# A recurrent stage of 128 steps written out without loops, with root, gate scaling and softmax made for two quads at once

## The chip, the cores and the metric

One core of one Trainium2 chip runs the whole program. The metric is device time in microseconds (us), from launch to the last result, as the median of several executions; lower is better. The profile covers one execution: its span runs from the first to the last instruction and is a little shorter than the device time of the same execution.

## The reference

The input x is 128 batches x 128 tokens x 128 channels, in float32, and adj a 128x128 weight matrix for each batch. Two blocks follow one another:

```python
def step(h, x):
    h = jnp.tanh(x @ Wx + h @ Wh + b)
...
x = x + gnn(layernorm(x), adj)      # gnn: agg = (beta / rowsum(adj)) x adj, then the scan of step over the 128 tokens
x = x + ffn(layernorm(x), ...)
# ffn: gate_logits = x @ gate_w + gate_b; top 2 of 16 experts, softmax over the two;
#      relu(x @ w1[e] + b1[e]) @ w2[e] + b2[e], weighted, added to x, layernorm, gamma, beta
```

The scan is a chain of 128 steps, and each step handles all 128 batches at once (the state h is a 128x128 tile).

## The kernel before, in words

The program has four stages one after the other in time: (1) statistics, scaling and aggregation with adj, by batches, up to about 78 us; (2) the recurrent stage, 78 to about 288 us, which this case is about; (3) a pass of the experts over the rows sorted by first choice; (4) a pass over the rows sorted by second choice.

**The recurrent stage** runs on all five engines, and four tokens make a *quad*, so there are 32 quads (`NQ`). Per quad:

- TensorE (`steps` L449 in the block that begins at L383). Step k of quad q waits for the tanh before it (`s_th`) and multiplies by Wh into a PSUM bank (L455). Behind the four steps other work is put in: behind step 0 the input part of the next quad (`fresh`, L446); behind step 1 `turn_h` of quad q-1, four transposes of h (L408); behind step 2 `count` of quad q-3 (five small matmuls on the one-hots, L437 to L440, which wait for `s_hot`) and then `logits` of quad q-2 (L425); behind step 3 `turn_x` of quad q-1, four transposes (L416, they wait for `s_x1`).
- ScalarE (`steps` L549): the tanh (L554), and behind step 0 the copy of the transposed x (`x1T_out` L529) and `tokens` (L546); behind step 1 `exps` and `sums` of quad q-3 (L535, L539, for the softmax; they wait for `s_dd`); behind steps 2 and 3 a part of the centring of w2.
- VectorE (`turn` L801): everything else of a quad, in 23 parts that are spread over three turns by a table of (part, lag). Turn q takes `tile_a` (L624: h transposed plus the residual x, waits for `s_ht`, for the load of x and for the slot's old scatters), `tile_b`, `tile_b2` (statistics of four tokens, L631, L638), `tile_b3`, `root_0` and eight small parts (one over the root of the variance, L645 to L680) of quad q-1; `gate_1` to `gate_5` (scaled logits, bias, largest values, their indices, one-hots; L693 to L730) of quad q-2; the softmax weights (L738, L742) and `place_1` to `place_3` (the row that each token goes to; L750 to L766) of quad q-3.
- GpSimd (`send` L328, scatter L222): four indirect DMAs a quad write the quad's rows to `rows_by_first` in DRAM. `send` waits for `tokens`, for the weights (`s_w1`) and for the places (`s_d`).
- SP loads the residual x of a quad (L256), four quads ahead: the load of quad q+4 is issued when `tile_a` of quad q is done. Between the loads of quads 4 to 7 and that of quad 8 it issues the filling of `rows_by_second`, w1, b1, gamma and beta.

The tile `st` has eight slots of a quad each: `tile_a` and `tokens` of quad q wait until the scatters of quad q-8 have landed. When the last places are known, VectorE works out tables for the expert passes (L820 to L856); when all engines are done with the stage's block, stage 3 starts.

The loops are these. `quads` (L233) writes the first 8 quads out and runs the other 24 as a hardware loop of 3 rounds with 8 quads each; VectorE, ScalarE and GpSimd use it, TensorE's own loop has 2 rounds between two written-out pieces. In the loop a wait against a number that depends on the round needs a register operation ahead of it, and `hold` puts one more wait on a constant in front.

```python
order = ((tile_a, 1), (soft_2, 3), (tile_b, 1), (soft_3, 3), (place_1, 3), (tile_b2, 1), (place_2, 3),
         (tile_b3, 1), (gate_1, 2), (root_0, 1), (place_3, 3), (sq_0, 1), (gate_2, 2),
         (ag_0, 1), (gate_3, 2), (in_0, 1), (gate_4, 2), (ou_0, 1), (sq_1, 1), (gate_5, 2), (ag_1, 1),
         (in_1, 1), (ou_1, 1))
```

In the profile L233 is the loop, and L222 the scatter of all stages.

Of the kernel before, what the change touches and what calls it, by code (L numbers as in the profile page):

```python
# [13 lines left out]
P = 128  # L14
# [3 lines left out]
UN = 4  # L18
GNN_EPS = 1e-7
# [15 lines left out]
def build(nc, x, adj, eW, Wx, Wh, b, gate_w, gate_b, w1, b1, w2, b2, gamma, beta, out):  # L35
# [11 lines left out]
    with ExitStack() as ctx:  # L47
# [73 lines left out]
        dd = fsb("dd", [P, 2, QUAD])  # L121
        ex = fsb("ex", [P, 2, QUAD])
        den = fsb("den", [P, 2, QUAD])
# [10 lines left out]
        ve2 = fsb("ve2", [P, 2, QUAD])  # L134
        root_y = fsb("root_y", [P, 2, QUAD])
        root_a = fsb("root_a", [P, 2, QUAD])
        root_b = fsb("root_b", [P, 2, QUAD])
        lgs = fsb("lgs", [P, 2, QUAD, NE])
        mx8 = fsb("mx8", [P, 2, QUAD, 8])
        ix8 = fsb("ix8", [P, 2, QUAD, 8], U32)  # L140
# [149 lines left out]
        def _(pool):  # L290
# [93 lines left out]
        def _(pe):  # L384
# [35 lines left out]
            def logits(q, u):  # L420
                pe.wait_ge(s_xe, q + 1)
                if beyond(q, 1):
                    pe.wait_ge(s_l1, q)
                for j in range(QUAD):
                    i = mm(ps_lg[:, j * NE:(j + 1) * NE], x1T[:, u % 2, j * P:(j + 1) * P], gwc[:, :],  # L425
# [23 lines left out]
            def steps(q, u):  # L449

                for k in range(QUAD):
# [29 lines left out]
            count(NQ - 3, UN - 3)  # L481
            logits(NQ - 2, UN - 2)
            turn_x(NQ - 1, SLOTS - 1)
            logits(NQ - 1, UN - 1)
            count(NQ - 2, UN - 2)
            count(NQ - 1, UN - 1)
# [9 lines left out]
        def _(act):  # L496
# [34 lines left out]
            def exps(q, u):  # L531
                act.wait_ge(s_dd, q + 1)
                if beyond(q, 2):
                    act.wait_ge(s_w1, q - 1)
                a(ex[:, u % 2, :], dd[:, u % 2, :], ACT.Exp).then_inc(s_ex, 1)  # L535

            def sums(q, u):
                act.wait_ge(s_ex, q + 1)
                a(den[:, u % 2, :], ex[:, u % 2, :], ACT.Identity, bias=unit[:, :]).then_inc(s_den, 1)  # L539
# [9 lines left out]
            def steps(q, u):  # L549
                for k in range(QUAD):  # L550
# [34 lines left out]
            quads(act, steps, SLOTS)  # L585
            exps(NQ - 3, UN - 3)
            sums(NQ - 3, UN - 3)
            x1T_out(NQ - 2, UN - 2)
            x1T_out(NQ - 1, UN - 1)
            exps(NQ - 2, UN - 2)  # L590
            sums(NQ - 2, UN - 2)
            exps(NQ - 1, UN - 1)
            sums(NQ - 1, UN - 1)
# [5 lines left out]
        def _(dve):  # L599
# [41 lines left out]
            def tile_b3(q, u):  # L641
                dve.wait_ge(s_pr, q + 1)
                if beyond(q, 2):
                    dve.wait_ge(s_r2, q - 1)
# [569 lines left out]
```

## Time and profile before

| | us |
|---|---|
| device time, median of 3 runs | 710.54 (709.33 to 710.82) |
| device time of the profiled execution | 710.99 |
| its span | 709.0 |
| recurrent stage: first tanh to last tanh | 77.89 to 260.84 |
| first and last scatter to `rows_by_first` begin | 97.29 and 283.59 |
| first instruction of stage 3 | 288.10 |

Busy shares of the whole span: TensorE matmuls 77%, weight loads 69%, VectorE 76%, ScalarE 58%, GpSimd 66%. The mean granted clock of TensorE is 0.888 of full speed. Shares over the whole span mix four stages with different limits, so for this change only views cut to the stage say something: who waits for whom, busy time by window, and instructions in order of time. In such a timeline the distance between the starts of two neighbours on one engine is what the first of them costs that engine, and it can be smaller than its duration, since neighbours overlap.

### The profile page before, as it was taken

The numbers are of one execution on the slowest core, as the hardware profiler recorded it, in microseconds if no ns is written. First come the engines' busy times: TensorE is split into PE (matmuls) and PEld (weight loads), VectorE is DVE, ScalarE is ACT, GpSimd is POOL, SyncE is SP. The second block draws the span as 40 slices with busy tenths as digits, with TensorE's granted clock in tenths as the row PEclk, the third lists the DMA queues.
The fourth block names the chain that finished last, engine by engine and source line by source line (L and its number), as shares of the span: only waits on it lengthen the run. The fifth ranks groups of instructions, "written<-read, shape, count | busy, mean of one in ns | idle before, by whom it ended". The sixth has DMA issues, their size and how long they took to land.

```text
span 709.0 us, 18043 instructions
## 1 busy us (share of the span) xinstructions
PE 544.5 (77%) x4140; PEld 486.8 (69%) x4140; DVE 539.0 (76%) x2791; ACT 407.8 (58%) x1345; POOL 466.6 (66%) x526
## 2 busy tenths in 40 slices
PE   1766789887888873399999999800799999999920
PEld 1655566665666652399999999800789999999920
DVE  5988599897997997288888888700299999999950
ACT  2889655454554540266666666500588888888810
POOL 3666647675765767067777777776067777777774
PEclk9989999897987985599999999955799999999975
DMA  8999649432332313379885665430997676664110
GB/s 216 282 281 282 158 147 278 143 104 75 96 94 84 97 49 114 80 210 334 258 251 192 202 190 185 150 149 28 294 328 231 191 215 202 208 203 142 49 49 7
DMA packets 115098, 121.40 MB, mean 171 GB/s; under 512 B 19017, under 2 KB 99613, under 8 KB 115008
## 3 DMA queue, kind: packets, MB, share of 16 engines
q1 hardware_dynamic: 95936, 76.79, 38.7%
q0 software_dynamic: 17920, 43.03, 16.7%
q8 instruction: 34, 0.56, 0.4%
q10 hardware_dynamic: 1152, 0.56, 0.3%
q14 instruction: 56, 0.46, 0.2%
HBM read 68.67 MB, written 55.90 MB: 176 GB/s over the span
## 4 chain that ended last, share of the span: by engine, by line
PE 38%; POOL 7%; ACT 7%; issue 4%; DMA 1%; DVE 1%; SPq 1%; POOLq 0%; ACTq 0%; DVEq 0%
PE bank L987 19%; PE bank L1003 15%; ACT hs L1055 4%; POOL rows_by_second L222 4%; POOL out_dram L222 3%; PE bank L976 3%; ACT xT L1036 2%; PE bank L1000 2%; DMA R<-rows_by_second 0%; DMA rows_by_second<-R 0%; DMA R<-rows_by_first 0%; ACT wr L1044 0%; SPq L912 0%; ACT L1064 0%; SPq L914 0%
## 5 line engine op out<-in xcount | busy, mean ns | idle before, releaser
L222 POOL DMA_INDIRECT rows_by_second<-R x144 | 146.2, 1015 | 62.2 <-issue 36.6
L222 POOL DMA_INDIRECT out_dram<-R x144 | 143.2, 994 | 66.7 <-issue 38.7
L1055 ACT ACTIVATE hs<-bank,wr 128x128 f32<-128x128 f32 x432 | 127.5, 368 | 86.7 <-PE bank L987 82.7
L1003 PE MATMUL bank<-W,hs 128*128 x1152 | 176.1, 289 | 0.0
L222 POOL DMA_INDIRECT rows_by_first<-st x128 | 125.3, 979 | 76.6 <-ACT st L546 40.2
L987 PE MATMUL bank<-xT,wr 128*128 128x128 f32 x1152 | 159.1, 282 | 7.2 <-ACT xT L1036 6.7
L1003 PEld LDWEIGHTS bank<-W,hs 128*128 128x128 f32 x1152 | 151.7, 192 | 3.5
L987 PEld LDWEIGHTS bank<-xT,wr 128*128 128x128 f32 x1152 | 143.1, 196 | 14.6 <-ACT xT L1036 13.4
L1124 DVE SCALAR_TENSOR_TENSOR R<-bank,R 128x128 f32<-128x128 f32 x288 | 87.6, 346 | 66.6 <-PE bank L1003 63.2
L1044 ACT COPY wr<-W1b 128x258 f32 x288 | 105.0, 427 | 14.7 <-PEq L858 14.7
L554 ACT ACTIVATE HT<-bank,bcol 128x128 f32<-128x128 f32 x128 | 46.7, 365 | 69.6 <-PE bank L455 65.7
L976 PE MATMUL bank<-ident,R 128*128 128x128 f32 x288 | 45.0, 281 | 54.0 <-DMA R<-rows_by_second 40.9
L976 PEld LDWEIGHTS bank<-ident,R 128*128 128x128 f32 x288 | 35.1, 146 | 54.7 <-DMA R<-rows_by_second 41.1
L1036 ACT COPY xT<-bank 128x512 f32<-128x512 f32 x72 | 42.9, 595 | 47.7 <-PE bank L976 47.7
L455 PEld LDWEIGHTS bank<-HT,Wh_sb 128*128 128x128 f32 x254 | 45.8, 212 | 35.0 <-ACT HT L554 29.7
L455 PE MATMUL bank<-HT,Wh_sb 128*128 128x128 f32 x254 | 62.3, 331 | 3.3 <-ACT HT L554 2.3
L1000 PE MATMUL bank<-b2s,sel 128*128 128x128 bf16 x288 | 63.2, 219 | 0.4 <-ACT hs L1055 0.3
L400 PE MATMUL bank<-aq,xs 128*128 128x128 f32 x256 | 42.2, 319 | 24.9 <-ACT xs L511 24.8
L400 PEld LDWEIGHTS bank<-aq,xs 128*128 128x128 f32 x256 | 36.4, 221 | 30.7 <-ACT xs L511 19.2
L1113 DVE TENSOR_SCALAR hs<-bank,wr 128x128 f32<-128x128 f32 x144 | 43.8, 346 | 10.3 <-PE bank L987 10.3
L1102 DVE TENSOR_SCALAR R<-R 128x128 f32<-128x128 f32 x144 | 42.2, 366 | 11.7 <-DMA R<-rows_by_first 11.7
L511 ACT ACTIVATE xs<-xq,scq 128x128 f32<-128x128 f32 x128 | 40.8, 391 | 10.0 <-POOL scq L325 9.1
(137 smaller groups left out, 875.4 us busy)
## 6 DMA issues: line engine op xcount, KB each, us to landing
R<-rows_by_second SPq DMA_DIRECT2D x144, 196.0 KB
R<-rows_by_first SPq DMA_DIRECT2D x144, 68.0 KB
xq<-in_x_dram SPq DMA_DIRECT2D x32, 256.0 KB, 4.0
aq<-in_adj_dram SPq DMA_DIRECT2D x32, 256.0 KB, 5.0
x2r<-in_x_dram SPq DMA_DIRECT2D x32, 256.0 KB, 2.9
rows_by_second<-filler SPq DMA_DIRECT2D x1, 3136.0 KB, 13.7
rows_by_second<-filler SPq DMA_DIRECT2D x16, 196.0 KB
rows_by_second<-R POOLq DMA_INDIRECT x144
```

The lines of the kernel that those rows point to most:

```text
L222: return nc.gpsimd.indirect_dma_start(dst, bass.IndirectOffsetOnAxis(ap=idx, axis=0), src, None, bounds_check=limit[n], oob_is_err=False)
L400: i = mm(ps_agg[u % 2][:, j * P:(j + 1) * P], xs[:, u % 2, j * P:(j + 1) * P], aq[:, u, j * P:(j + 1) * P], start=True, stop=True)
L455: mm(ps_rnn[u % 2][:, k * P:(k + 1) * P], Wh_sb[:, :], HT[:, h, ((k - 1) % QUAD) * P:((k - 1) % QUAD + 1) * P], start=False, stop=True, sk ...
L554: a(HT[:, u % 2, k * P:(k + 1) * P], ps_rnn[u % 2][:, k * P:(k + 1) * P], ACT.Tanh, bias=bcol[:, :]).then_inc(s_th, 1)
L976: i = nc.tensor.transpose(ps_z[:, j * P:(j + 1) * P], R[:, u, j, C_Z:C_Y], ident[:, :])
L987: i = mm(ps_h[c][h][:, (j % 2) * P:(j % 2 + 1) * P], wr[:, u % 2, j, c * P:(c + 1) * P], xT[:, u % 2, j * P:(j + 1) * P], start=True, stop ...
L1000: mm(o, sel[:, bass.ds(e[k], 1), :].rearrange("p o m -> p (o m)"), b2s[:, :], start=True, stop=False, skip_group_check=True)
L1003: i = mm(o, hs[:, h, c, k * P:(k + 1) * P], W2[:, bass.ds(e[k], 1), c, :].rearrange("p o f -> p (o f)"), start=False, stop=c == 1, skip_gr ...
L1036: nc.scalar.copy(xT[:, u % 2, :], ps_z[:, :]).then_inc(e_xe, 1)
L1044: i = nc.scalar.copy(wr[:, u % 2, j, :], W1b[:, bass.ds(e, 1), :].rearrange("p o f -> p (o f)"))
L1055: i = a(hs[:, h, c, k * P:(k + 1) * P], ps_h[c][h][:, k * P:(k + 1) * P], ACT.Relu, bias=wr[:, u % 2, 2 * h + k, F + c:F + c + 1])
L1124: i = v.scalar_tensor_tensor(out=y, in0=ps_o[h][:, k * P:(k + 1) * P], scalar=R[:, u, j, w:w + 1], in1=y if r else R[:, u, j, C_Z:C_Y], op ...
```

## The change

TensorE, ScalarE, VectorE and GpSimd write out all 32 quads of the stage, with no loop. `tile_b3`, the root, `gate_1` to `gate_3`, the difference for the softmax (now `apart`) and the softmax weights are made once for a pair of quads, with tiles twice as wide. VectorE's table of parts is replaced by two kinds of turn, `even` and `odd`: the root of a pair is made in the even turn t = 2p+2, the gate of the pair in the odd turn 2p+3, the indices and one-hots of quad q in turn q+3 (before: q+2), the places of quad q in turn q+4 (before: q+3). TensorE takes the logits behind step 1 instead of step 2, and the counts of quad q-4 instead of q-3. ScalarE's exp and sum are made once a pair, in even quads. Cut to its core:

```diff
@@ pool
-                pool.wait_ge(s_w1, q + 1)
+                pool.wait_ge(s_w1, q // 2 + 1)
...
-            def turn(q, u):
-                if beyond(q, 3):
-                    send(q - 3, (u - 3) % SLOTS)
-            quads(pool, turn, SLOTS)
-            for k in range(3):
-                send(NQ - 3 + k, SLOTS - 3 + k)
+            for q in range(NQ):
+                send(q, q % SLOTS)
@@ pe
-                if beyond(q, 1):
-                    pe.wait_ge(s_l1, q)
+                if beyond(q, 2):
+                    pe.wait_ge(s_l1, q // 2)
...
-                    if k == 2 and beyond(q, 3):
-                        count(q - 3, u - 3)
-                    if k == 2 and beyond(q, 2):
+                    if k == 1 and beyond(q, 2):
                         logits(q - 2, u - 2)
+                    if k == 2 and beyond(q, 4):
+                        count(q - 4, u - 4)
...
-            for u in range(SLOTS):
-                steps(u, u)
-            with pe.Fori(1, NQ // SLOTS - 1) as J:
-                for u in range(SLOTS):
-                    steps(SLOTS * J + u, u)
-            for u in range(SLOTS):
-                steps(NQ - SLOTS + u, u)
+            for q in range(NQ):
+                steps(q, q % SLOTS)
@@ act
-                    if k == 1 and beyond(q, 3):
-                        exps(q - 3, u - 3)
-                        sums(q - 3, u - 3)
+                    if k == 1 and q % 2 == 0 and q > 3:
+                        exps(q // 2 - 2)
+                        sums(q // 2 - 2)
...
-            quads(act, steps, SLOTS)
+            for q in range(NQ):
+                steps(q, q % SLOTS)
@@ dve (root, gate_1 to gate_3, apart, soft_2, soft_3: one call a pair, 8 columns for 4)
-                v.tensor_scalar(ve2[:, u % 2, :], st[:, u, :, C_RSTD], LN_EPS, None, ALU.add).then_inc(s_v2, 1)
+                v.tensor_scalar(ve2[:, p % 2, :], two(p, C_RSTD), LN_EPS, None, ALU.add).then_inc(s_v2, 1)
...
-                v.tensor_tensor(lgs[:, h, :, :], ps_lg[:, 0:QUAD * NE].rearrange("p (i e) -> p i e", i=QUAD),
+                v.tensor_tensor(lgs[:, p % 2, :, :], ps_lg[:, 0:PAIR * NE].rearrange("p (i e) -> p i e", i=PAIR),
...
-            quads(dve, turn, SLOTS)
-            for q in range(NQ, NQ + 3):
-                turn(q, q % SLOTS)
+            def odd(t):
+                p = (t - 3) // 2
+                one(tile_a, t - 1)
+                one(tile_b, t - 1)
+                pair(gate_1, p)
+                one(tile_b2, t - 1)
+                pair(gate_2, p)
+                one(place_1, t - 4)
+                pair(gate_3, p)
+                one(place_2, t - 4)
+                pair(apart, p)
+                one(gate_4, t - 3)
+                one(place_3, t - 4)
+                one(gate_5, t - 3)
+
+            def even(t):
+                p = (t - 2) // 2
+                one(tile_a, t - 1)
+                one(tile_b, t - 1)
+                one(gate_4, t - 3)
+                one(tile_b2, t - 1)
+                one(gate_5, t - 3)
+                pair(tile_b3, p)
+                one(place_1, t - 4)
+                pair(root_0, p)
+                pair(soft_2, p - 1)
+                pair(sq_0, p)
+                one(place_2, t - 4)
+                pair(ag_0, p)
+                pair(soft_3, p - 1)
+                pair(in_0, p)
+                one(place_3, t - 4)
+                pair(ou_0, p)
+                pair(sq_1, p)
+                pair(ag_1, p)
+                pair(in_1, p)
+                pair(ou_1, p)
+
+            for t in range(0, NQ + 4, 2):
+                even(t)
+                odd(t + 1)
```

How this moves instructions, at three places. TensorE, one quad of the stage before, from the transposes of h behind step 1 to the input part of the next quad (L455 is a step, L437 to L440 the count, L425 the logits, L416 the transposes of x):

```order
L408 MATMUL bank<-ident,HT 128x128 [waits s_x1]
L408 MATMUL bank<-ident,HT 128x128 x3
L455 MATMUL bank<-HT,Wh_sb 128x128 [waits s_th]
L437 MATMUL bank<-hot,ones 128x160 [waits s_hot]
L438 MATMUL bank<-hot,tri 128x128
L440 MATMUL bank<-hot,ones 128x96
L440 MATMUL bank<-hot,ones 128x64
L440 MATMUL bank<-hot,ones 128x32
L425 MATMUL bank<-gwc,x1T 128x16 [waits s_l1,s_xe]
L425 MATMUL bank<-gwc,x1T 128x16 x3
L455 MATMUL bank<-HT,Wh_sb 128x128 [waits s_th]
L416 MATMUL bank<-ident,st 128x128 [waits s_xe,s_x1]
```

The same piece of a quad in the change (L454 is a step, L424 the logits, L436 to L439 the count, L414 the transposes of x):

```order
L406 MATMUL bank<-ident,HT 128x128 [waits s_x1]
L406 MATMUL bank<-ident,HT 128x128 x3
L424 MATMUL bank<-gwc,x1T 128x16 [waits s_l1,s_xe]
L424 MATMUL bank<-gwc,x1T 128x16 x3
L454 MATMUL bank<-HT,Wh_sb 128x128 [waits s_th]
L436 MATMUL bank<-hot,ones 128x160 [waits s_hot]
L437 MATMUL bank<-hot,tri 128x128
L439 MATMUL bank<-hot,ones 128x96
L439 MATMUL bank<-hot,ones 128x64
L439 MATMUL bank<-hot,ones 128x32
L454 MATMUL bank<-HT,Wh_sb 128x128 [waits s_th]
L414 MATMUL bank<-ident,st 128x128 [waits s_xe,s_x1]
```

The logits now stand ahead of step 2 rather than ahead of step 3, and the count stands alone behind step 2. VectorE, the gate inside a turn of the loop before (L710 finds the largest values, L718 their indices, L722 is the difference; root parts between them):

```order
L663 REGISTER_ALU
L664 TENSOR_TENSOR root_b<-root_a,ve 128x4 [waits s_root]
L710 MAX mx<-lgs 128x8 [waits s_const,s_l2,s_hot]
L710 MAX mx<-lgs 128x8 x3
L670 REGISTER_ALU
L671 SCALAR_TENSOR_TENSOR root_a<-root_b 128x4 [waits s_root]
L718 MAX_INDEX ix<-mx,lgs 128x8 [waits s_mx,s_const]
L718 MAX_INDEX ix<-mx,lgs 128x8 x3
L722 TENSOR_TENSOR dd<-mx 128x4 [waits s_ex]
L678 REGISTER_ALU
L680 SCALAR_TENSOR_TENSOR root_y<-root_a,root_y 128x4 [waits s_root]
```

VectorE in the change, the gate inside an odd turn (L753, L764 and L769 are the places, L708 the largest values, L717 the difference, L724 the indices, L733 the one-hots):

```order
L697 TENSOR_TENSOR lgs<-lgs,gb_bc 128x128 [waits s_l1]
L753 TENSOR_TENSOR posr<-bank,posr 128x160 [waits s_sel,s_cnt]
L708 MAX mx<-lgs 128x8 [waits s_l2,s_hot]
L708 MAX mx<-lgs 128x8 x7
L764 TENSOR_TENSOR picked<-posr,hot 128x128 [waits s_d,s_pos]
L717 TENSOR_TENSOR dd<-mx 128x8 [waits s_ex,s_mx]
L724 MAX_INDEX ix<-mx,lgs 128x8 [waits s_mx]
L724 MAX_INDEX ix<-mx,lgs 128x8 x3
L769 TENSOR_REDUCE st<-picked 128x4x2 [waits s_sel]
L733 TENSOR_TENSOR hot<-ix,iota_e 128x128 [waits s_cnt,s_ix]
```

The register operations are gone, the gate has eight maxima in one go, and no root part stands in the odd turn. All of the root is in the even turn, whose end is (L661 to L677 are the last root parts, L616 is `tile_a` of the next turn):

```order
L745 TENSOR_TENSOR st<-st,ex 128x8 [waits s_red]
L668 SCALAR_TENSOR_TENSOR root_a<-root_b 128x8 [waits s_root]
L769 TENSOR_REDUCE st<-picked 128x4x2 [waits s_sel]
L677 SCALAR_TENSOR_TENSOR root_y<-root_a,root_y 128x8 [waits s_root]
L654 TENSOR_TENSOR root_a<-root_y 128x8 [waits s_root]
L661 TENSOR_TENSOR root_b<-root_a,ve 128x8 [waits s_root]
L668 SCALAR_TENSOR_TENSOR root_a<-root_b 128x8 [waits s_root]
L677 SCALAR_TENSOR_TENSOR st<-root_a,root_y 128x8 [waits s_root]
L616 TENSOR_TENSOR st<-bank,x2r 128x4x128 [waits s_sct2,s_x22,s_ht]
```

The last four root parts follow each other with nothing between them.

## Rows read from the trace of the kernel before

**Rows 1.** Who waited for whom, 78 to 285 us: us in total, times, longest.

```profile
POOL rows_by_first L222 <- ACT st L546: 40.2, 23, 14.6
...
ACT ex L535 <- DVE dd L722: 26.5, 24, 3.1
```

**Rows 2.** Busy by window: PE, PEld, DVE, ACT, POOL, then clock, DMA share, GB/s.

```profile
136.00:159.00 23.00, 18.88 (x127) 14.40 (x127) 21.66 (x167) 12.32 (x46) 16.40 (x17) 0.97 0.33 98
78.00:261.00 183.00, 153.07 (x947) 115.95 (x946) 163.71 (x1192) 93.79 (x343) 113.13 (x114) 0.89 0.39 116
```

**Rows 3.** Timeline of VectorE, one turn: start, duration, line, operation, shapes, [idle before].

```profile
133.90 0.69 DVE L624 TENSOR_TENSOR st<-bank,x2r 128x512 f32<-128x512 f32 x1
...
134.63 0.87 DVE L631 BATCH_NORM_STATS2 bnb<-st 128x6 f32<-128x128 f32 x4
...
135.48 0.32 DVE L750 TENSOR_TENSOR posr<-bank,posr 128x160 f32<-128x160 f32 x1
...
136.00 0.29 DVE L761 TENSOR_TENSOR picked<-posr,hot 128x128 f32<-128x128 f32 x1
136.22 0.16 DVE L645 TENSOR_SCALAR ve<-st 128x4 f32<-128x4 f32 x1
136.29 0.21 DVE L693 TENSOR_TENSOR lgs<-bank,st 128x64 f32<-128x64 f32 x1
136.42 0.15 DVE L650 TENSOR_SCALAR root_y<-ve 128x4 int32<-128x4 int32 x1
...
137.10 0.41 DVE L710 MAX8 mx<-lgs 128x8 f32<-128x16 f32 x4
...
137.61 0.09 DVE L718 MATCH_VALUE_LOAD ix<-mx,lgs 128x8 f32 x1
...
138.21 0.14 DVE L722 TENSOR_TENSOR dd<-mx 128x4 f32<-128x4 f32 x1
...
138.54 0.29 DVE L730 TENSOR_TENSOR hot<-ix,iota_e 128x128 bf16<-128x128 uint32 x1
138.75 0.15 DVE L664 TENSOR_TENSOR root_b<-root_a,ve 128x4 f32<-128x4 f32 x1
138.94 0.16 DVE L671 SCALAR_TENSOR_TENSOR root_a<-root_b 128x4 f32<-128x4 f32 x1
...
139.33 0.69 DVE L624 TENSOR_TENSOR st<-bank,x2r 128x512 f32<-128x512 f32 x1
```

**Rows 4.** Timeline of VectorE: `tile_a` of quads 3, 8 and 15.

```profile
98.70 0.69 DVE L624 TENSOR_TENSOR st<-bank,x2r 128x512 f32<-128x512 f32 x1
...
128.33 0.69 DVE L624 TENSOR_TENSOR st<-bank,x2r 128x512 f32<-128x512 f32 x1 [2.13 <-DMA x2r<-in_x_dram]
...
171.26 0.69 DVE L624 TENSOR_TENSOR st<-bank,x2r 128x512 f32<-128x512 f32 x1 [3.31 <-issue]
```

**Rows 5.** Timeline of GpSimd: the first scatter, the first of quad 6, the last.

```profile
97.29 1.25 POOL L222 DMA_INDIRECT rows_by_first<-st  x1 [14.59 <-ACT st L546]
...
132.14 0.97 POOL L222 DMA_INDIRECT rows_by_first<-st  x1 [2.88 <-ACT st L546]
...
283.59 0.97 POOL L222 DMA_INDIRECT rows_by_first<-st  x1 [0.30 <-issue]
```

**Rows 6.** Timelines of ScalarE and weight loads, quad 8: tanh 0, 1, 3, then the next quad's.

```profile
117.09 0.37 ACT L554 ACTIVATE HT<-bank,bcol 128x128 f32<-128x128 f32 x1 [0.29 <-PE bank L455]
...
118.17 0.37 ACT L554 ACTIVATE HT<-bank,bcol 128x128 f32<-128x128 f32 x1
118.59 0.30 PEld L455 LDWEIGHTS bank<-HT,Wh_sb 128*128 128x128 f32 x2 [0.26 <-ACT HT L554]
...
120.06 0.97 PEld L425 LDWEIGHTS bank<-gwc,x1T 128*128 128x128 f32 x8
...
121.49 0.37 ACT L554 ACTIVATE HT<-bank,bcol 128x128 f32<-128x128 f32 x1 [1.05 <-PE bank L455]
...
122.44 0.37 ACT L554 ACTIVATE HT<-bank,bcol 128x128 f32<-128x128 f32 x1 [0.29 <-PE bank L455]
```

More of the change, by code:

```diff
@@ L18 @@
 UN = 4
+PAIR = 2 * QUAD
+NPAIR = NQ // 2
 GNN_EPS = 1e-7
@@ L584, in _ @@
             agg_out(NQ - 1, UN - 1)
-            quads(act, steps, SLOTS)
-            exps(NQ - 3, UN - 3)
-            sums(NQ - 3, UN - 3)
+            for q in range(NQ):
+                steps(q, q % SLOTS)
             x1T_out(NQ - 2, UN - 2)
             x1T_out(NQ - 1, UN - 1)
[L590 to L593, printed above, removed]
+            for p in range(NPAIR - 2, NPAIR):
+                exps(p)
+                sums(p)
             act.wait_ge(starts, 1)
@@ L639, in tile_b2, with two, tile_b3, root_0 @@
                 i.then_inc(s_pr, 1)
[L641 to L644, printed above, removed]
[L645 to L650 removed]
+            def two(p, c):
+                s = 2 * p % SLOTS
+                return st[:, s:s + 2, :, c].rearrange("p u j -> p (u j)")
+            def tile_b3(p):
+                dve.wait_ge(s_pr, 2 * p + 2)
+                if p > 1:
+                    dve.wait_ge(s_r2, p - 1)
+                v.tensor_scalar(ve2[:, p % 2, :], two(p, C_RSTD), LN_EPS, None, ALU.add).then_inc(s_v2, 1)
+            def root_0(p):
+                dve.wait_ge(s_v2, p + 1)
+                v.tensor_scalar(root_y[:, p % 2, :].bitcast(I32), ve2[:, p % 2, :].bitcast(I32), -0.5, ROOT_BITS,
                                 ALU.mult, ALU.add).then_inc(s_root, 1)
             def square(n):
[L654 to L656 removed]
+                def part(p):
+                    h = p % 2
+                    dve.wait_ge(s_root, 8 * p + 4 * n + 1)
                     v.tensor_tensor(root_a[:, h, :], root_y[:, h, :], root_y[:, h, :], ALU.mult).then_inc(s_root, 1)
@@ L675, in outer, with part @@
             def outer(n, scale):
-                def part(q, u):
-                    h = u % 2
-                    dve.wait_ge(s_root, 8 * q + 4 * n + 4)
+                def part(p):
+                    h = p % 2
+                    dve.wait_ge(s_root, 8 * p + 4 * n + 4)
                     y = root_y[:, h, :]
-                    i = v.scalar_tensor_tensor(out=st[:, u, :, C_RSTD] if n else y, in0=root_a[:, h, :],
+                    i = v.scalar_tensor_tensor(out=two(p, C_RSTD) if n else y, in0=root_a[:, h, :],
                                                scalar=5 * scale ** 4, in1=y, op0=ALU.add, op1=ALU.mult)
@@ L699, in gate_2, with gate_3 @@
+            def gate_2(p):
+                h = p % 2
+                dve.wait_ge(s_l1, p + 1)
                 v.tensor_tensor(lgs[:, h, :, :], lgs[:, h, :, :],
-                                gb_bc[:, :].rearrange("p (o e) -> p o e", o=1).broadcast_to([P, QUAD, NE]),
+                                gb_bc[:, :].rearrange("p (o e) -> p o e", o=1).broadcast_to([P, PAIR, NE]),
                                 ALU.add).then_inc(s_l2, 1)
-            def gate_3(q, u):
-                h = u % 2
-                if beyond(q, 2):
-                    hold(dve, s_hot, q - 1)
-                hold(dve, s_l2, q + 1)
-                for j in range(QUAD):
+            def gate_3(p):
+                h = p % 2
+                if p > 1:
+                    dve.wait_ge(s_hot, 2 * p - 2)
+                dve.wait_ge(s_l2, p + 1)
+                for j in range(PAIR):
@@ L710, in gate_3, with apart @@
                     i = v.max(mx8[:, h, j, :], lgs[:, h, j, :])
                 i.then_inc(s_mx, 1)
+            def apart(p):
+                h = p % 2
+                dve.wait_ge(s_mx, p + 1)
+                if p > 1:
+                    dve.wait_ge(s_ex, p - 1)
+                v.tensor_tensor(dd[:, h, :], mx8[:, h, :, 1], mx8[:, h, :, 0], ALU.subtract).then_inc(s_dd, 1)
             def gate_4(q, u):
-                h = u % 2
-                hold(dve, s_mx, q + 1)
-                for j in range(QUAD):
+                h = q // 2 % 2
+                dve.wait_ge(s_mx, q // 2 + 1)
+                for j in range(q % 2 * QUAD, q % 2 * QUAD + QUAD):
@@ L797, in _, with one, pair @@
             link(v.memset(hot[:, :, 0:2 * NE], 0.0))
-            def turn(q, u):
-                order = ((tile_a, 1), (soft_2, 3), (tile_b, 1), (soft_3, 3), (place_1, 3), (tile_b2, 1), (place_2, 3),
-                         (tile_b3, 1), (gate_1, 2), (root_0, 1), (place_3, 3), (sq_0, 1), (gate_2, 2),
-                         (ag_0, 1), (gate_3, 2), (in_0, 1), (gate_4, 2), (ou_0, 1), (sq_1, 1), (gate_5, 2), (ag_1, 1),
-                         (in_1, 1), (ou_1, 1))
-                for part, lag in order:
-                    if beyond(q, lag) and not (isinstance(q, int) and q - lag >= NQ):
-                        part(q - lag, (u - lag) % SLOTS)
-            quads(dve, turn, SLOTS)
-            for q in range(NQ, NQ + 3):
-                turn(q, q % SLOTS)
+            def one(part, q):
+                if 0 <= q < NQ:
+                    part(q, q % SLOTS)
+            def pair(part, p):
+                if 0 <= p < NPAIR:
+                    part(p)
+            def odd(t):
[37 more added lines that the diff above has]
+                odd(t + 1)
             dve.wait_ge(s_d, NQ)
```

98 lines of the change are left out of this document (44 added, 54 removed).

## The prediction

> **What bounds the kernel now.** I read who waits for whom in the stage first. GpSimd's scatters wait longest for something of their own quad [rows 1], and ScalarE's exp, which stands between two tanh, waits 26.5 us for the difference that VectorE makes. Both point at VectorE. The windows confirm it: in an undisturbed stretch VectorE is busy 21.66 of 23 us (94%), TensorE 18.88, GpSimd 16.40 [rows 2]. The reader is to see that nothing else comes near 94%. The timeline of one turn then gives the period: `tile_a` to `tile_a` is 139.33 - 133.90 = 5.43 us without a gap [rows 3]; over seven turns of the loop it is 171.26 - 128.33 = 42.93, less a gap of 3.31, so 5.66 a turn [rows 4]. That gap has no releaser but "issue" and stands where the loop jumps back; there are two such jumps, since the loop has three rounds. A third gap, 2.13 us, is not the loop's: `tile_a` of quad 8 waits for its load of x [rows 4].
>
> The end of the stage is the last scatter, which begins at 283.59 [rows 5]. A scatter takes 0.97 and the issue behind it 0.30, so 1.27 each and 5.1 a quad. 128 of them need 163 us, but 186.3 lie between the first start and the last [rows 5]; GpSimd is therefore hungry for some 24 us, and that is what this change can win. It is also all that it can win: GpSimd's own work is not touched.
>
> **The new period of VectorE.** I price parts by the distance of starts [rows 3]: `tile_a` until `tile_b` can begin 0.73, `tile_b` with one softmax part 0.85 (0.78 alone), `place_1` with `tile_b2` 0.52, `place_2` 0.20, `tile_b3` 0.07, `gate_1` 0.13, four maxima 0.41, `gate_4` 0.60, one-hots 0.21. `place_3` isn't priced by a row; it is of `place_2`'s kind, 0.20. A small part that needs nothing fresh costs 0.07; one that needs the result of its neighbour costs 0.19 to 0.20 (138.75 to 138.94). Twice the width costs `gate_1` 64 elements more; 512 elements take 0.69 and 64 take 0.21, so 1.07 ns each, and `gate_1` becomes 0.20, `gate_2` 0.21. Eight maxima are 0.70. Eight columns for four in the root cost four elements, nothing that counts.
>
> Even turn: 0.73 + 0.78 + 0.60 + 0.52 + 0.21 + 0.07 = 2.91 up to `root_0`. Then `root_0` to `sq_0` 0.20, `sq_0` 0.07, `place_2` 0.20, `ag_0` to `in_0` 0.20, `in_0` 0.07, `place_3` 0.20: 3.85. Then five root parts with nothing between them, 5 x 0.19 = 0.95: **4.8**. Odd turn: 0.73 + 0.78 + 0.20 + 0.52 + 0.21 + 0.70 + 0.20 + 0.07 + 0.60 + 0.20 + 0.21 = **4.4**. A pair takes 9.2, a turn 4.6. Register operations and the extra constant waits drop out, and the two jumps with them (3.3 each).
>
> **The chain of tanh.** Step 0 to 1 takes 118.17 - 117.09 = 1.08, a step with little behind it 122.44 - 121.49 = 0.95 [rows 6]. The logits move behind step 1: they hold the weight loads for 0.97, of which 0.26 were idle there anyway, so this step takes 0.95 + 0.97 - 0.26 = 1.66. Step 2 keeps the count alone, 0.95, step 3 0.95. Sum 4.64 a quad. exp and sum fit behind tanh 1, once in two quads; the difference they need is made in the odd turn before, over 1 us early. The chain and VectorE now need the same, 4.6 to 4.7 with some friction. Both are below the 5.1 of GpSimd: **GpSimd becomes the bound**, and what is late next is its first scatter and any hole in its supply.
>
> **When the scatters can begin.** Places come a turn later. Quads 0 to 3 of the chain cannot be much faster than before; from 90.5 on they take 4.64, so `tile_a` of quad 3 starts at about 96.6 instead of 98.70 [rows 4]. Turn 4 hands over the places of quad 0 at its 3.9: the first scatter starts at 100.6, 3.3 later than the 97.29 of before [rows 5].
>
> Then comes the load of quad 8. SP issues it behind the filling and w1 to beta, all of it behind `tile_a` of quad 3. From that `tile_a` to the one of quad 8 it is 128.33 - 98.70 = 29.6 [rows 4]. I take this distance as fixed, since SP and the DMA queues set it; it could be shorter at least by the 0.6 to 1 us that is VectorE's, and longer by a few us if scatters and code get in between. VectorE and the chain are there 6 us early and stand still: `tile_a` of quad 8 at 96.6 + 29.6 = 126.2. The same turn hands over the places of quad 5 at its 4.2, so 130.5. GpSimd is through with quad 4 before 127 and stands for some 3.5 us. Before, quad 6 started at 132.14 at this point [rows 5]; now it is quad 5 at 130.5.
>
> From here on a turn (4.7) is shorter than four scatters (5.1), so supply stays ahead. 27 quads are 108 scatters, the last one starts at 130.5 + 107 x 1.277 = 267.1. Two deductions, both allowances: 1.2 us for single slow scatters (the first of the stage took 1.25 instead of 0.97 [rows 5]); and hunger in the first turns after 130.5, while the lead is small, 0.8. The last start is then 269.1 instead of 283.59: **-14.5**. What VectorE does behind the last places (the tables) is hidden behind the last scatters, because those places are ready at 131 + 25 x 4.7 + 4 = 253, 16 us ahead of the last start; without that cover it would lie on the path in full. The way from the last scatter into stage 3, and stages 1, 3 and 4, stay as they are.
>
> **A rule against the change.** An ungrouped turn costs 5.4 [rows 3], more than GpSimd's 5.1, so grouping pays: 25 turns x 0.3 would be lost without it. The Trainium skill (Perfetto Trace Analysis, Optimizing Scalar/DVE Operations) says that grouping helps if the engine is saturated, but where it isn't and only leaves holes in others, "breaking up instructions may allow work to be completed sooner". By the rows VectorE is saturated before the change and isn't after it, so both halves apply: the later places alone cost four scatters, 5.1 us, at the hole at 130.5. By the rule's second half alone the sum would be -19.6, by the rows it is -14.5.
>
> **Rivals.**
> 1. *VectorE or the chain still sets the pace, at 5.1 to 5.7.* For: the mean granted clock of the stage is 0.89, 0.97 in the good window [rows 2], and at half clock the input part and logits grow into the chain; waits now couple two quads. Against: both sums stand 0.5 below. At 5.4 a turn the last places are ready at 131 + 25 x 5.4 + 4.2 = 270, the last scatter starts 3.8 later, -9.6; with 5.7, where only the jumps are won, -2. Time 697 to 709, middle 701. Chance 0.20.
> 2. *The hole at quad 8 is smaller or absent.* If its load comes when VectorE asks for it, GpSimd runs from 100.6 without a hole and the last start is 100.6 + 127 x 1.277 + 2 = 265, or 262.8 with nothing lost: 690 to 692. For: SP's part of the 29.6 isn't shown to be fixed. Against: the wait was a real one before. Chance 0.10.
> 3. *Slower: written-out code does not arrive in time.* A jump cost 3.31 [rows 4]; code that is run once must all be fetched, and if engines stood still for such a gap again and again, the chain would pay each. The result turns to slower when the turns behind quad 8 take over 5.85 on average (131 + 25 x 5.85 + 4.2 + 3.8 = 285), 1.2 more than summed, one gap of 3.3 every third turn. At one every second turn, 6.3 a turn, it is +12, 722. Against: quads 0 to 7, and the first round of the loop, are code that is run for the first time, and up to quad 15 the trace shows only the DMA's gap [rows 4]. Chance 0.04.
>
> **How the numbers follow.** Forecast 0.66, rivals 0.20, 0.10 and 0.04. The profiled execution took 710.99, 0.45 above the median of 710.54; 710.99 - 14.5 = 696.5, against the median 696.0. The forecast's own range comes from the fixed distance (-1 to +3), the hunger (0 to 2) and the friction: 694 to 700. To hold 8 in 10 it reaches down towards rival 2 and up into rival 1: 692.5 to 702.5. A measurement of this kernel tells about 0.2% from no change, 1.4 us. Slower takes rival 3 at 0.04; the same takes the end of rival 1 where next to nothing is won, 0.02; faster 0.94.
>
> **What would show it.** Starts of scatters 1.28 apart from about 130 to the end, with no wait for places or softmax; before 130 one hole of some 3 us. The first scatter near 100.6, `tile_a` of quad 8 near 126 with a DMA as its releaser, the last scatter near 269. VectorE's turns 4.8 and 4.4 where nothing holds them, its busy share well below 94%. Tanh 1 to tanh 2 1.6 to 1.7. No "issue" gap of 3 us. I am wrong if scatters after 131 still wait for places (rival 1), if the hole at quad 8 is missing or twice as long, or if gaps with no releaser recur (rival 3).

## The result and the profile after

| | before | after |
|---|---|---|
| device time, median | 710.48 (709.24 to 710.82, 6 runs) | 693.51 (692.24 to 695.36, 6 runs) |
| ratio to before, 95% interval | 1 | 0.9766 (0.9749 to 0.9783) |
| device time of the profiled execution | 710.99 | 693.63 |
| its span | 709.0 | 691.8 |
| first, last scatter to `rows_by_first` begin | 97.29, 283.59 | 100.89, 266.59 |
| first to last | 186.30 | 165.70 |
| first copy of stage 3 (ScalarE) | 288.67 | 271.67 |

The kernel became 17.0 us faster (median against median), and the last scatter begins 17.0 us earlier. From the first copy of stage 3 to the last instruction both kernels take 420 us (709.0 - 288.67 = 420.3 and 691.8 - 271.67 = 420.1), so the gain lies ahead of stage 3.

Who waits for whom, changed kernel, 78 to 275 us (engine, what it makes and its line, releaser: us in total, times, longest), which answers to [rows 1]:

```profile
ACT HT L548 <- PE bank L454: 53.4, 94, 4.7
...
POOL rows_by_first L224 <- issue: 36.3, 119, 0.3
...
POOL rows_by_first L224 <- ACT st L540: 19.2, 3, 18.6
...
ACT st L540 <- DMA rows_by_first<-st: 10.3, 8, 3.1
...
DVE st L616 <- DMA x2r<-in_x_dram: 4.7, 1, 4.7
...
POOL rows_by_first L224 <- DVE st L769: 3.8, 6, 2.3
```

Of 127 scatters behind the first, 119 now follow the one before them with only the 0.30 of issue (36.3 in 119). The row of 19.2 is nearly all the wait ahead of the first scatter (18.6), and of the 3.8 for places one hole is 2.3. A new row has appeared: ScalarE's `tokens` waits 10.3 us, 8 times, until old scatters have landed. From 182 us on the other engines are so far ahead that the eight slots of `st` are full, and GpSimd holds them back. In the kernel before, GpSimd waited for the others.

The name of the releaser in these rows (`ACT st`, L540 here and L546 in [rows 1]) can't be taken at its word. `send` waits for three semaphores, and `tokens` of the same quad has long run: for quad 0 of the changed kernel at 77.86, for quad 10 of the kernel before at 131.38. What came last is `place_3`. The two engines of the kernel before at quad 10:

```profile
153.31 0.28 DVE L766 TENSOR_REDUCE st<-picked 128x8 int32<-128x128 f32 x1
...
154.40 0.97 POOL L222 DMA_INDIRECT rows_by_first<-st  x1 [0.86 <-ACT st L546]
```

`place_3` ends at 153.59 and the scatter begins 0.81 later. In the kernel before this distance is 0.80 to 1.15 for all quads from 0 to 28, and for nearly all of them GpSimd stands until their places are there. In the changed kernel it is 0.99 at quad 0 and 0.81 at quad 5 (behind the hole), and then it grows: 3.7 at quad 10, 10.2 at quad 20, 17.7 at quad 31. So the places are ready ever earlier than they are needed.

What follows is GpSimd's timeline (start, duration, [idle time before and its releaser]): the first scatter, the hole at quad 5, the last three. They answer to [rows 5].

```profile
100.89 1.25 POOL L224 DMA_INDIRECT rows_by_first<-st  x1 [18.63 <-ACT st L540]
...
125.64 0.97 POOL L224 DMA_INDIRECT rows_by_first<-st  x1 [0.30 <-issue]
128.90 0.97 POOL L224 DMA_INDIRECT rows_by_first<-st  x1 [2.29 <-DVE st L769]
130.17 0.97 POOL L224 DMA_INDIRECT rows_by_first<-st  x1 [0.30 <-issue]
...
264.04 0.97 POOL L224 DMA_INDIRECT rows_by_first<-st  x1 [0.30 <-issue]
265.31 0.97 POOL L224 DMA_INDIRECT rows_by_first<-st  x1 [0.30 <-issue]
266.59 0.97 POOL L224 DMA_INDIRECT rows_by_first<-st  x1 [0.31 <-issue]
```

VectorE's timeline: `tile_a` of quad 3, of quad 8 (with the wait for its load), and the next three, which bound an odd, an even and an odd turn, without their inner parts. They answer to [rows 4] and [rows 3].

```profile
96.01 0.69 DVE L616 TENSOR_TENSOR st<-bank,x2r 128x512 f32<-128x512 f32 x1 [0.40 <-PE bank L406]
...
123.64 0.69 DVE L616 TENSOR_TENSOR st<-bank,x2r 128x512 f32<-128x512 f32 x1 [4.66 <-DMA x2r<-in_x_dram]
...
128.88 0.69 DVE L616 TENSOR_TENSOR st<-bank,x2r 128x512 f32<-128x512 f32 x1 [0.60 <-PE bank L406]
...
133.60 0.69 DVE L616 TENSOR_TENSOR st<-bank,x2r 128x512 f32<-128x512 f32 x1
...
137.94 0.69 DVE L616 TENSOR_TENSOR st<-bank,x2r 128x512 f32<-128x512 f32 x1
```

Even turn 133.60 - 128.88 = 4.72, odd turn 137.94 - 133.60 = 4.34, without a gap of "issue" anywhere.

Four tanh of one quad on ScalarE, and the first of the next (tanh to tanh, as in [rows 6]):

```profile
150.06 0.37 ACT L548 ACTIVATE HT<-bank,bcol 128x128 f32<-128x128 f32 x1 [0.35 <-PE bank L454]
...
151.08 0.37 ACT L548 ACTIVATE HT<-bank,bcol 128x128 f32<-128x128 f32 x1
...
152.63 0.37 ACT L548 ACTIVATE HT<-bank,bcol 128x128 f32<-128x128 f32 x1 [1.19 <-PE bank L454]
...
153.58 0.37 ACT L548 ACTIVATE HT<-bank,bcol 128x128 f32<-128x128 f32 x1 [0.29 <-PE bank L454]
...
154.58 0.37 ACT L548 ACTIVATE HT<-bank,bcol 128x128 f32<-128x128 f32 x1 [0.35 <-PE bank L454]
```

A quad takes 1.02 + 1.55 + 0.95 + 1.00 = 4.52; the 1.55 is the step with the logits behind it.

Busy time by window (length, then busy us of PE, PEld, DVE, ACT, POOL, granted clock, DMA share, GB/s); the first window is the one of [rows 2], the second the hole:

```profile
136.00:159.00 23.00, 21.67 (x158) 17.47 (x159) 22.56 (x173) 14.43 (x52) 17.51 (x19) 1.00 0.40 123
```

```profile
122.00:128.00 6.00, 3.62 (x11) 2.58 (x12) 4.15 (x31) 0.94 (x3) 3.70 (x4) 0.50 0.74 252
159.00:231.00 72.00, 62.95 (x456) 50.28 (x454) 66.45 (x480) 41.21 (x146) 54.93 (x57) 1.00 0.34 101
```

VectorE is busy 98% in the window of [rows 2] and still 92% in the last. So a busy share doesn't tell who bounds here: a VectorE that runs ahead and fills slots is as busy as one that everybody waits for. The waits tell it, and the distance from `place_3` to the scatter.

### The profile page after: what moved, and what is told of

Same layout as the page of the kernel before. It is cut to its first block, busy times and chain, and to the rows that moved or that the text cites. A ratio compares the mean times of both kernels' runs of the same rounds, so it can differ in the third digit from the quotient of the medians.

```text
span 691.8 us, 17131 instructions
## 1 busy us (share of the span) xinstructions
PE 526.6 (76%) x4140; PEld 478.3 (69%) x4140; DVE 511.9 (74%) x2551; ACT 401.5 (58%) x1313; POOL 467.5 (68%) x526
## 4 chain that ended last, share of the span: by engine, by line
PE 38%; ACT 7%; POOL 7%; issue 4%; DVE 2%; DMA 1%; SPq 1%; POOLq 0%; ACTq 0%; DVEq 0%
PE bank L1028 19%; PE bank L1044 15%; POOL rows_by_second L224 5%; ACT hs L1096 5%; PE bank L1017 3%; ACT xT L1077 3%; POOL out_dram L224 2%; PE bank L1041 2%; DMA R<-rows_by_second 1%; DVE R L1197 0%; DVE R L1165 0%; DMA rows_by_second<-R 0%; DMA R<-rows_by_first 0%; DVE R L1189 0%; DVE fst L1175 0%
## 5 line engine op out<-in xcount | busy, mean ns | idle before, releaser
L224 POOL DMA_INDIRECT rows_by_first<-st x128 | 126.0, 984 | 59.3 <-issue 36.3
L454 PE MATMUL bank<-HT,Wh_sb 128*128 128x128 f32 x254 | 58.9, 314 | 15.3 <-ACT HT L548 14.6
L454 PEld LDWEIGHTS bank<-HT,Wh_sb 128*128 128x128 f32 x254 | 41.0, 192 | 42.7 <-ACT HT L548 42.1
```

The costliest lines, as they stand in the source:

```text
L224: return nc.gpsimd.indirect_dma_start(dst, bass.IndirectOffsetOnAxis(ap=idx, axis=0), src, None, bounds_check=limit[n], oob_is_err=False)
L454: mm(ps_rnn[u % 2][:, k * P:(k + 1) * P], Wh_sb[:, :], HT[:, h, ((k - 1) % QUAD) * P:((k - 1) % QUAD + 1) * P], start=False, stop=True, sk ...
```

## The experiments

The expectations speak of four theories. **A**: VectorE set the pace before (turns of 5.4 to 5.7 and the jumps), and after it GpSimd's scatters, 5.1 a quad, once the places are there. **B**: GpSimd bounds both. **C**: VectorE, or the chain of tanh, bounds both. **D**: the pairing is what pays, not the loops.

The experiments ran on four chips. Two of them ran every kernel much slower (the kernel before 904 us instead of 710); what they gave stands apart below. Times elsewhere are from chips where the kernel before takes 709.7 to 710.5.

### More work for GpSimd

A memset of 128 x 392 numbers ahead of the four scatters of each quad, in the kernel before (`before_pool_more`) and in the changed one (`after_pool_more`). In both it waits, with `hold`, for the memset of the quad before.

```diff
+                g.memset(spare[:, :], 0.0).then_inc(s_spare, 1)
                 for j in range(QUAD):
                     scatter(dram_a.ap()
```

> The kernel before with one more GpSimd instruction a quad (a memset of 128x392, 0.42 us where the trace has one) ahead of each quad's scatters. Theory A (before: VectorE's 5.66 us a turn bounds, GpSimd's 5.1 a quad has room): 5.5 still fits, only the last few sends, which run back to back, pay; +1 to +3 us on 710.5. Theory B (GpSimd bounds before as well as after): 32 x 0.42 = +13. Theory C (VectorE or the chain bounds before and after): as A here.

> The changed kernel with the same extra memset a quad. Theory A (the scatters are the bound from quad 5 on): 27 quads x 0.42 to 0.45 = +11 to +12.5 us on 693.5. Theory C (VectorE or the chain still sets the pace): +1 to +3.

Measured: before 709.29 (ratio 0.9992, 0.9975 to 1.0008), no change clear of noise, where theory A gave +1 to +3; changed kernel 700.77 (0.9869, 0.9852 to 0.9887), 7.3 more than without the memset. B falls with the first number, C with the second. In the profiled execution of the former the quads at the end do pay (5.41 instead of 5.11 between them), but the last scatter begins at 281.25, 2.3 earlier than without the memset: `tile_a` of quad 8 came at 126.80 instead of 128.33, and several turns behind it were shorter. Why is open. GpSimd's timeline of the changed kernel with the memset:

```profile
181.48 0.97 POOL L226 DMA_INDIRECT rows_by_first<-st  x1 [0.30 <-issue]
182.43 0.47 POOL L339 MEMSET spare<- 128x392 f32 x1
183.06 0.97 POOL L226 DMA_INDIRECT rows_by_first<-st  x1 [0.17 <-POOL spare L339]
```

The 7.3 is less than theory A's figure (+11 to +12.5) because the memset was mis-priced: it begins while the scatter still counts as busy and lies partly in the 0.30 of issue, so it moves the next scatter from 1.28 to 183.06 - 181.48 = 1.58, by 0.30 and not by its duration of 0.47. What it cost the quads ahead of quad 5 the hole there swallowed: the quads' distance at the hole is 5.89 instead of 7.09. From quad 5 on the quads take 5.40 to 5.54, where they take 5.11 to 5.25 without it.

### More work for VectorE

One operation of 384 columns behind the statistics of each quad.

```diff
+                v.tensor_scalar(spare[:, 0:3 * P], aq[:, 0, 0:3 * P], 1.0, None, ALU.mult)
```

> The kernel before with one more VectorE instruction a turn (a product of 128x384 with one, estimated at 0.25 to 0.45 us from 0.22 for 128x128 in the trace) behind tile_b. Theory A and C: each turn is longer by it, 32 x 0.25 to 0.45 = +8 to +14 us. Theory B (GpSimd bounds): under +3.

> The changed kernel with the same extra VectorE instruction a turn. Theory A: turns of 4.53 grow to 4.8 to 5.0, still under the 5.15 of four scatters; only the way to the first scatter and to quad 5 behind the hole pays, 0 to +2 us. Theory C: +8 to +14, as in the kernel before.

Measured: before 717.96 (1.0130, 1.0099 to 1.0161), +7.7, a little under what was expected; changed kernel 695.07 (0.9799, 0.9774 to 0.9824), +1.6 by the medians and +2.3 by the ratios, with an interval that overlaps that of the plain one. Its last scatter in the profiled execution (693.02, the fastest of its four, which reach up to 696.63):

```profile
265.37 0.97 POOL L225 DMA_INDIRECT rows_by_first<-st  x1 [0.30 <-issue]
```

It is not later than 266.59, though most of its turns grew to 4.5 to 4.8 and 5.0 to 5.2. In the kernel before the same operation made ordinary turns 5.8 to 6.3 and moved the last scatter from 283.59 to 291.21. The operation takes 0.34 us and moves its follower on VectorE by 0.26 (in the changed kernel it begins at 129.12, the next at 129.38), so 32 of them are 8.3 us of VectorE's time. They cost 7.6 before; after, none at the last scatter of this execution, and 0 to about 4 us by the times. The first turns of the kernel before got theirs nearly for nothing: `tile_a` of quad 8 begins at 128.51 instead of 128.33, and its wait of 2.13 for the load is gone. Both halves of theory A are borne out: the bound passed from VectorE to GpSimd.

### The loops alone, and the wait for quad 8 taken away

`before_unrolled_third` is the kernel before with the stage written out, and nothing paired or moved; the waits on a constant that `hold` makes are still in it.

```diff
-            quads(dve, turn, SLOTS)
-            for q in range(NQ, NQ + 3):
+            for q in range(NQ + 3):
                 turn(q, q % SLOTS)
```

(and likewise for TensorE, ScalarE and GpSimd). `after_b1_late_again` is the changed kernel with the two loads of b1 (8 KB each, in single numbers) at the end of SP's part of the stage:

```diff
-            for c in range(2):
-                sp.dma_start(W1b[:, :, F + c], b1.rearrange("e (c f) -> c f e", c=2)[c],
-                             allow_slow_non_contiguous=True).then_inc(r_w, 16)
...
+            for c in range(2):
+                sp.dma_start(W1b[:, :, F + c], b1.rearrange("e (c f) -> c f e", c=2)[c],
+                             allow_slow_non_contiguous=True).then_inc(r_w, 16)
             sp.wait_ge(starts, 1)
```

> The kernel before with the recurrent stage written out, nothing grouped. On a chip where the kernel before takes about 710: theory A (VectorE bound before, a jump cost 3.3 each) expects turns of 5.4 without the two gaps, a hole at quad 8 as in the kernel before, last scatter at about 274 to 279, 701 to 706; theory D (the pairing is what pays) expects the same or less, 704 to 708; if GpSimd already runs without hunger, the last scatter is at 267 and the time 693 to 695. On a chip where the kernel before takes about 904: 895 to 898 as in the two earlier runs.

> The changed kernel with the two slow loads of b1 issued at the end of SP's part of the stage. On a chip where the kernel before takes about 710: theory A expects no wait of VectorE for the load of x at quad 8 and no hole at quad 5 of the scatters, last scatter at about 264.3 instead of 266.6, time 2.3 less than the changed kernel, about 691; a theory that GpSimd is not what bounds expects no change. On a chip where the kernel before takes about 904: 902 as before.

Measured on one chip: written out 696.4 (0.9808, 0.9788 to 0.9829), b1 late 692.08 (0.9751, 0.9732 to 0.9771); before 709.66. The first is 5 us below the lower end that theory A gave, and its last scatter (270.41) lies ahead of the 274 to 279: I had not taken the loop's own cost in ordinary turns into account. Who released `tile_a` (its 32 instructions), in the kernel before and in the one written out:

```profile
L624 DVE TENSOR_TENSOR st<-bank,x2r x32: 690/692/694, 84.2 to 265.2; 128x512 f32<-128x512 f32 x32
its engine sat idle before it (us, times) until:
  issue: 7.8, 8
  DMA x2r<-in_x_dram: 2.1, 1
```

```profile
L619 DVE TENSOR_TENSOR st<-bank,x2r x32: 690/692/693, 83.7 to 251.5; 128x512 f32<-128x512 f32 x32
its engine sat idle before it (us, times) until:
  DMA x2r<-in_x_dram: 2.7, 1
```

"issue" is gone. Turns are 5.31 nearly everywhere (range behind quad 9: 5.30 to 5.77), where the loop has 5.43 to 5.86 and two of 9.2. From `tile_a` of quad 8 to that of quad 31 it is 136.8 us before and 251.50 - 127.70 = 123.8 written out: the two jumps give 7.8 of the 13.0, the other 21 turns 0.25 each. The constant waits can't be a part of that 0.25, since both kernels have them; the register operations of the loop are gone, but no run shows them by themselves. But 5.31 is still more than 5.1, and VectorE still bounds: for the quads 2 to 28 the first scatter begins 0.80 to 0.84 after `place_3` has ended. The waits, 78 to 275 us:

```profile
POOL rows_by_first L222 <- ACT st L540: 29.6, 25, 14.6
...
PEld bank L436 <- DVE hot L725: 26.8, 27, 3.0
...
ACT ex L529 <- DVE dd L717: 24.8, 28, 3.4
```

ScalarE waits for the softmax difference as long as in [rows 1]; with the pairs that row is down to 3.8, once.

The kernel with b1 late has no wait for x at quad 8 (`tile_a` begins at 120.00), and GpSimd has no hole (its first scatter and the last two):

```profile
101.98 1.25 POOL L224 DMA_INDIRECT rows_by_first<-st  x1 [20.23 <-ACT st L540]
...
263.74 0.97 POOL L224 DMA_INDIRECT rows_by_first<-st  x1 [0.30 <-issue]
265.02 0.97 POOL L224 DMA_INDIRECT rows_by_first<-st  x1 [0.30 <-issue]
```

| | first scatter | last | between | time against before |
|---|---|---|---|---|
| before | 97.29 | 283.59 | 186.30 | |
| written out only | 96.79 | 270.41 | 173.62 | -13.3 |
| changed kernel | 100.89 | 266.59 | 165.70 | -17.0 |
| changed, b1 late | 101.98 | 265.02 | 163.04 | -17.6 |
| 127 x 1.277 (no hunger) | | | 162.2 | |

So of the 17 us the writing out gives 13, and everything else in the change 3 to 4: the pairs with the later places, but also the logits behind step 1 and VectorE's `hold` waits, of which `gate_3` and `gate_4` have none any more. No run on a usual chip takes these apart. The 3 to 4 are a difference of two: from quad 6 on the changed kernel needs 6.5 less (132.56 against 139.07, 25 quads), and it comes to quad 6 2.7 later (134.03 against 131.34). D falls. With b1 late GpSimd runs without hunger, and the 2.7 less between first and last is what was expected (2.3). In time it is hardly to be told from the changed kernel (the intervals overlap), since its first scatter came 1.1 later. I don't know why: its `tile_a` of quad 3 was already at 97.09 instead of 96.01, before any difference in the programs plays. Its median is the lowest of all versions.

### On two other chips

There the kernel before took 903.67 and 903.79. Ratios to it:

| | ratio, 95% interval |
|---|---|
| `before_unrolled`, and `_again` on the other chip | 0.9913 (0.9885 to 0.9941), 0.9935 (0.9911 to 0.9958) |
| `unrolled_b1_late_plain`, and `_again` | 0.9903 (0.9868 to 0.9937), 0.9917 (0.9883 to 0.9951) |
| `after_b1_late` | 0.9972 (0.9943 to 1.0002) |
| `after_logits_step2` | 1.0091 (1.0053 to 1.0129) |

`unrolled_b1_late_plain` is the written-out kernel before with b1 late and without the constant waits of `tile_b2`, `gate_3` and `gate_4`. `after_logits_step2` puts the logits back behind step 2 in the changed kernel:

```diff
-                    if k == 1 and beyond(q, 2):
-                        logits(q - 2, u - 2)
                     if k == 2 and beyond(q, 4):
                         count(q - 4, u - 4)
+                    if k == 2 and beyond(q, 2):
+                        logits(q - 2, u - 2)
```

> The kernel before with the loops of its recurrent stage written out and nothing else (same table of parts, one quad at a time, logits behind step 2, places three turns behind). Theory A: a turn falls from 5.66 to the 5.3 of the quads that were written out before, both jumps go; quad 6 starts at 132 as before, last places 25 turns x 5.3 later, last scatter about 267: -16 to -17 us on 710.5, that is the whole gain of the change, since pairing brings VectorE below a bound that is GpSimd's and its later places cost a quad at the hole. Theory D (pairing is what pays): the two jumps alone, -6 to -8.

> The changed kernel with the two slow loads of b1 (15 us of issue on SP) moved behind the loads of x, which takes away most of what stands ahead of the load of quad 8. Theory A: the 2.3 us hole ahead of quad 5's scatters closes, last scatter at 100.9 + 127 x 1.287 = 264.3: -2.3 us on 693.5 (-1.5 to -3). If the scatters were not the bound: the chain gains its 4.7 us wait, -4 to -5, or nothing.

> The kernel before, loops written out, b1 late, and the double waits of tile_b2, gate_3 and gate_4 made single. Places stay three turns behind, so scatters start at 97.3. Theory A: VectorE's turn is 5.1 to 5.3, near the 5.15 of four scatters; last scatter 261 to 265, so 688 to 692 us, 2 to 5 below the changed kernel. If single quads cannot reach 5.3 a turn: 693 or more.

> The changed kernel with the logits back behind step 2, behind the count. Theory A: the chain keeps its 4.5 to 4.7 a quad and isn't the bound; 0 +- 0.7 us on 693.5. If where the logits stand matters (they would wait for the count's one-hots, and the gate's difference would come late): +3 or more.

> The same kernel as before_unrolled, on another chip, since the first ran all kernels a quarter slower. Theory A: turns of 5.3, first scatter at 97, last scatter about 267, so 693 to 695 us where the kernel before takes 710.5, level with the changed kernel. Theory D (pairing is what pays): 702 to 704.

> The same kernel as unrolled_b1_late_plain, on another chip. Theory A: no hole ahead of quad 6, turns of 5.1, first scatter at 96.5 to 97.3, last one 261 to 264: 688 to 691 us where the kernel before takes 710.5. If single quads stay at 5.3 a turn: last scatter 264 to 266, 691 to 693.

None of the times is where it was expected. Here everything behind some 100 us takes longer, also the expert passes that no kernel touched (570 to 575 us instead of 420), while the first scatter is where it always is. A piece of VectorE's timeline, `before_unrolled`:

```profile
105.46 0.16 DVE L652 TENSOR_TENSOR root_a<-root_y 128x4 f32<-128x4 f32 x1 [2.49 <-remote]
...
106.88 0.16 DVE L666 SCALAR_TENSOR_TENSOR root_a<-root_b 128x4 f32<-128x4 f32 x1 [0.98 <-DVE root_b L659]
```

```profile
78.00:300.00 222.00, 175.37 (x974) 138.09 (x974) 169.73 (x1260) 96.03 (x348) 116.94 (x119) 0.78 0.31 96
```

Each of these two parts needs only its neighbour's result on the same engine, and waits 2.5 and 1.0 us; in the same place of a usual chip the distance is 0.2. VectorE is busy 76% and TensorE's granted clock 0.78. What stops the engines is open. On these chips the order turns round: written out alone is 0.7 to 0.9% faster than the kernel before, and the changed kernel with b1 late is not told from it. The gain of the change is shown for chips of the usual kind only.

The logits may matter. On the same chip `after_logits_step2` is 1.2% (some 11 us) slower than `after_b1_late`, and its last scatter begins at 332.30 instead of 320.20; the place of b1, the other difference between the two, gave 1.4 us on a usual chip. The expectation was 0, or +3 and more if their place counts. So a part of the 3 to 4 us above can be the logits' new place; this, and what the constant waits cost, stays open, since the plain changed kernel didn't run on these chips and the two variants didn't run on a usual one.

## Why the prediction was right, point by point

Forecast 696.0 in a range of 692.5 to 702.5, measured 693.51.

**VectorE bounds before; GpSimd can win its hunger and no more**: shown, by the memset that cost nothing before and 7.3 after, and the operation that cost 7.7 before and 1.6 after. The hunger fell from 24 us to 165.7 - 162.2 = 3.5.

**The new turns**: 4.8 and 4.4 forecast, 4.72 and 4.34 measured. Pricing by the distance of starts, 0.07 for an independent small part and 0.19 to 0.20 for a dependent one, held to 2%. **The chain**: 4.64 forecast, 4.52 measured; the step with the logits is 1.55 instead of 1.66, which the runs don't explain further.

**The first scatter**: 100.6 forecast, 100.89 measured, and this was luck in part. `tile_a` of quad 3 came at 96.01, 0.6 earlier than the 96.6 of the sum. The way from there to the scatter took 4.88 instead of 4.0: the sum let the scatter begin as soon as VectorE hands over the places, and put nothing for the way to GpSimd. `place_3` ended at 99.90, which is the 3.9 of the sum, and the scatter began 0.99 later. The two errors cancel.

**The load of quad 8** is the term that was mis-sized most. I took its distance from `tile_a` of quad 3 as fixed at 29.6, and it was 27.6: 123.64 instead of 126.2. SP's queue in both kernels (start, time the issue took), before and after:

```profile
104.29 17.27 SPq L278 DMA_DIRECT2D W1b<-in_L_ffn_b_dram  x2
...
123.75 5.78 SPq L256 DMA_DIRECT2D x2r<-in_x_dram  x5
```

```profile
101.27 15.19 SPq L280 DMA_DIRECT2D W1b<-in_L_ffn_b_dram  x2
...
118.97 11.12 SPq L258 DMA_DIRECT2D x2r<-in_x_dram  x6
```

The issue of b1 is the piece that shrank, by 2.1; why is open. So `tile_a` of quad 8 was 2.6 earlier than forecast, but quad 5 began at 128.90 instead of 130.5, only 1.6 earlier. The missing way to GpSimd took the other 1.0: the 4.2 of the sum is where `place_3` begins (127.82), it ends at 128.09, and the scatter follows 0.81 later.

**The two allowances**: slow scatters 1.2, measured 266.59 - 128.90 - 107 x 1.277 = 1.05; hunger behind the hole 0.8, measured none. Then the last start: 269.1 less 1.6, 0.8 and 0.15 is 266.6, which is what was measured. The whole difference between forecast (-14.5) and result (-17.0) is in these three, and the 1.6 is itself 2.6 less 1.0. The last places were ready at 245.04 instead of 253, 22 us ahead of the last scatter, so the tables stay well hidden: the last four turns, which take up no new quad after the first of them, took 11.5 us together up to there (`tile_a` of quad 31 begins at 233.59), where I had counted 4.7 for each.

**The rule against the change**: written out but ungrouped, the kernel has turns of 5.31, not 5.4, so grouping (with what else changed beside it) was worth 6.5 us from quad 6 on instead of the 7.5 I gave it. The later places took back 2.7 of it, not 5.1: being a quad behind does cost 5.1, but the scatters behind the hole began at 128.90 instead of the 131.34 of the written-out kernel, since the load of quad 8 came sooner. The Trainium skill (Perfetto Trace Analysis, Optimizing Scalar/DVE Operations) says that grouping can improve throughput if the engine is saturated. The rows agree: VectorE was, and a turn fell from 5.31 to 4.53. No run tests its other half, the breaking up where the engine isn't saturated; the rows show only that the first scatter came later with the pairs, at 100.89 instead of 96.79. By the second half alone the sum was -19.6, which would mean that going without the pairs is the faster way. It isn't: without them the last scatter comes 13.2 earlier than in the kernel before, with them 17.0.

**The rivals**: behind quad 5 neither VectorE nor the chain set the pace of the scatters (rival 1). The hole was there, at 2.0 us beyond the usual distance instead of 3.5, and the run with b1 late is rival 2 made: forecast for it 690 to 692 with a last start of 262.8 to 265, measured 692.08 and 265.02, at the upper end of both. No gap of "issue" recurred (rival 3).

**A sign that was wrong**: I wrote that VectorE's busy share would fall well below 94%, and it is 98% in the same window. The forecast stands on the period (4.53 against 5.1), and the engine uses the difference to run ahead until slots are full. The sign to look for was the wait of `tokens` for a DMA, which I hadn't named.

## What to carry to other kernels

Ask first which engine's instructions still wait once the slack is gone. A wait for several semaphores can bear the wrong name: look when the named work ran. Then add a small operation to each suspect, in both kernels, and see which moves the end. A hardware loop can cost more than its jump: here two jumps were 7.8 us and the other turns in the loop another 5 on the saturated engine. Price a hand-over from one engine to another too: here 0.8 to 1.0 us from the end of VectorE's part to the start of the scatter. Where a group of parts is made larger and later, count the gain over the turns behind the next hole that stays, and the delay at that hole.

## What was not expected of the hardware

- The time SP needs to issue a load is not the load's own. With b1 out of the way, the small load of gamma behind w1 took 7.37 us to issue instead of 1.59, and the x loads started at 111.21 instead of 118.97, only 7.8 of the 15.2 earlier. The DMA share was 1.05 over 102 to 110 in that run, and 0.70 over 116 to 119 in the changed kernel, where gamma took the 1.59. That the queue behind SP was full of what had been issued before is my reading; no run shows it.
- TensorE waited 3.7 us for `tile_a` of quad 8, and its granted clock was 0.50 over 122 to 128 (the row above), the 1.2 GHz level. In the kernel before, whose `tile_a` of quad 8 waited until 128.33, it was 0.90 over 122 to 128 and 0.65 over 128 to 136. From 128 to 231 it was 1.00 in the changed kernel, 0.92 in the one written out only and 0.86 in the kernel before.
- Two chips ran the same program 27% slower from about 100 us on, with single engines standing for 1 to 2.5 us though what the code makes them wait for was done on the same engine.
